# A four-layer graph network: rows of the sources found by comparison instead of a map in memory

## The reference, cut to what matters

```python
x = _layernorm(x + L0(x))   # attention over 8 heads: k[src], q[dst], softmax over edges of one dst, sum of v[src]
x = _layernorm(x + L1(x))   # two graph convolutions, with self loops and degree norm
x = _layernorm(x + L2(x))   # GAT, 4 heads: softmax over the edges of one dst, sum of h[src], elu
x = _layernorm(x + L3(x))   # two relational convolutions, 10 relations, mean per relation
```

## Time and profile before

| | us |
|---|---|
| median of 3 runs (lowest, highest) | 2712.64 (2708.06, 2718.84) |
| the profiled execution's own time | 2743.0 |
| its span | 2741.1 |
| busy in the span: PE, DVE, POOL, ACT | 2165.8, 2091.5, 1721.6, 1461.9 |

### The profile page before, as it was taken

One profiled execution on the slowest core, in us unless ns is written; L12 is line 12 of the kernel. 1 busy time (PEld: TensorE's weight loads), 2 busy tenths in 40 slices (PEclk: granted clock), 3 DMA queues, 4 the chain that ended last, 5 costly groups with the idle time before them and its releaser, 6 DMA issues. The chain is left out here.

```text
span 2741.1 us, 52605 instructions
## 1 busy us (share of the span) xinstructions
PE 2165.8 (79%) x12429; PEld 1663.7 (61%) x12429; DVE 2091.5 (76%) x7133; ACT 1461.9 (53%) x4917; POOL 1721.6 (63%) x1824
## 2 busy tenths in 40 slices
PE   2888888544878776999676999667769999899996
PEld 1766667333656665887564898456646666555553
DVE  4788888423879996887798396678868888688886
ACT  1455556233667775666454586378854444333332
POOL 3888888687877885664886687233334444355554
PEclk9999999766888997999999698788889999999998
DMA  5566666532545544554675455334432323211221
GB/s 94 173 213 211 211 206 205 110 78 66 178 156 189 177 154 162 170 173 152 189 215 185 125 183 165 99 124 129 138 122 76 84 80 84 71 51 55 57 57 31
DMA packets 294159, 369.90 MB, mean 135 GB/s; under 512 B 64976, under 2 KB 148696, under 8 KB 293858
## 3 DMA queue, kind: packets, MB, share of 16 engines
q1 hardware_dynamic: 261858, 315.33, 36.3%
q0 software_dynamic: 32000, 51.21, 7.8%
HBM read 160.78 MB, written 207.00 MB: 134 GB/s over the span
## 5 line engine op out<-in xcount | busy, mean ns | idle before, releaser
L1708 PE MATMUL phase_p_w<-phase_w_rel,phase_rowsT 128*128 128x512 f32 (+1 forms) x1200 | 510.9, 528 | 9.9 <-ACT phase_rowsT L1761 9.8
L384 PE MATMUL phase_p_h<-W2c,phase_g 128*128 128x128 f32 x1568 | 233.2, 311 | 169.9 <-ACT phase_g L339 145.5
L1789 DVE SCALAR_TENSOR_TENSOR phase_added<-phase_p_w,relation,phase_added 128x128 f32<-128x128 f32 x1200 | 350.0, 340 | 22.6 <-PE phase_p_w L1708 20.8
L324 ACT ACTIVATE phase_sq<-phase_y 128x512 f32<-128x512 f32 x294 | 186.2, 633 | 311.8 <-POOL phase_y L457 290.9
L384 PEld LDWEIGHTS phase_p_h<-W2c,phase_g 128*128 128x128 f32 x1568 | 219.9, 224 | 182.3 <-ACT phase_g L339 156.8
L656 POOL DMA_INDIRECT phase_rows<-X,src_row x200 | 192.2, 961 | 217.9 <-PE phase_p_T L1716 167.6
L978 PE MATMUL phase_p_sum<-phase_whole,phase_link 128*128 128x128 f32 (+2 forms) x792 | 183.7, 316 | 130.2 <-ACT phase_whole L1100 64.0
L656 POOL DMA_INDIRECT phase_rows<-H,src_row x200 | 193.3, 967 | 136.0 <-PE phase_p_T L1716 110.1
L345 DVE TENSOR_REDUCE phase_ss<-phase_sq 128x4 f32<-128x512 f32 x294 | 195.5, 665 | 73.8 <-ACT phase_sq L324 69.5
L1708 PEld LDWEIGHTS phase_p_w<-phase_w_rel,phase_rowsT 128*128 128x128 f32 x1200 | 189.5, 193 | 86.3 <-issue 41.1
L978 PEld LDWEIGHTS phase_p_sum<-phase_whole,phase_link 128*128 128x128 f32 x792 | 128.7, 204 | 160.5 <-ACT phase_whole L1100 78.9
(11 more groups left out here) (235 smaller groups left out, 6976.1 us busy)
## 6 DMA issues: line engine op xcount, KB each, us to landing
H<-phase_h SPq DMA_DIRECT2D x196, 256.0 KB, 3.3
X<-phase_x SPq DMA_DIRECT2D x196, 256.0 KB, 3.2
phase_same<-same_keys SPq DMA_DIRECT2D x175, 256.0 KB
phase_xT<-in_x_columns SPq DMA_DIRECT2D x98, 256.0 KB, 3.6
Z<-phase_x SPq DMA_DIRECT2D x98, 256.0 KB
phase_x<-X SPq DMA_DIRECT2D x98, 256.0 KB
out<-phase_o SPq DMA_DIRECT2D x98, 256.0 KB
H<-R SPq DMA_DIRECT2D x50, 256.0 KB, 2.4
```

The lines of the kernel that those rows point to most:

```text
L324: act.activation(self.buf(dst, g)[:, :, :], self.buf(src, g)[:, :, :], ACT.Square).then_inc(self.S[dst], 1)
L384: last = self.nc.tensor.matmul(self.P["p_h2"][:, t, :], self.buf(f"g{k}", g)[:, t, :], self.W["W2c"][:, k, :], start=(k == 0), stop=(k == 1))
L1708: nc.tensor.matmul(p_w[(PARTS * (t % UNROLL) + n) % BANKS][:, 0:b - a, :], rowsT[v][:, :], w[:, a:b, :], start=True, stop=True).then_inc(s ...
L1789: nc.vector.scalar_tensor_tensor(out=added[v][r % 2][:, :], in0=p_w[(PARTS * (t % UNROLL) + n) % BANKS][:, r % RG, :], scalar=plane(D["rel ...
```

## The change

The map goes, with its scatters, its gathers and the `slot_row` table. The sources are stored once more as floats. A new stage `source_rows`, ahead of `attention_messages`, computes `src_row` on the chip. For 512 sources at a time it loads them broadcast over 101 partitions. POOL turns the first 100 partitions into a 0/1 *step matrix*: has the tile t a first key not above the source? PE multiplies this matrix, with the plain source in the last partition, by a table of the differences of keys between neighbouring tiles and a last row of -1. The product holds, for each source, the 128 keys of the one tile in which it would stand, minus the source; a second product with a column of ones counts the tiles passed. DVE compares the first product with zero, multiplies by the ordinals 1 to 128 and takes the maximum: the last matching slot, or 0. Six small operations at the end make `src_row` of it.

The slots of dense work are dealt out anew: 112 in `source_rows` (28 steps of four), 218 in `attention_messages` as before, 24 instead of 48 in the first `weights_of_edges`, and 81 instead of 169 in `attention_rows`. In `over_all_tiles`, which all pipelined stages use except the relation ones, the step now comes before its slots.

```diff
 def over_all_tiles(step, places, dense):
     for k, slots in enumerate(places):
+        step(k)
         for i in slots:
             dense(i)
-        step(k)
...
+                sp.wait_ge(s["rows_converted"], 3)
+                sp.dma_start(io["src_f"].rearrange("(t e) -> t e", e=F), src_f[:, :]).then_inc(s["dst_stored"], 16)
                 sp.wait_ge(s["marks_full"], 2)
                 for table, marks in ((io["link_rows"], link_rows), (io["back_rows"], back_rows)):
                     sp.dma_start(table, marks[:, :]).then_inc(s["marks_stored"], 16)
-                sp.wait_ge(s["dst_stored"], 16)
+                sp.wait_ge(s["dst_stored"], 32)
...
-                sp.wait_ge(s["node_made"], 1)
-                sp.dma_start(io["row_of"].rearrange("(p n) a -> p (n a)", p=125), node[:, :]).then_inc(s["node_stored"], 16)
-                sp.wait_ge(s["node_stored"], 16)
...
-                pool.iota(node[:, :], pattern=[[1, N // 125]], base=0, channel_multiplier=N // 125).then_inc(s["node_made"], 1)
                 pool.memset(beside[:, :, :], -1).then_inc(s["beside_cleared"], 1)
-                pool.iota(D["slot_row"][:, :], pattern=[[F, T]], base=N, channel_multiplier=1)
...
+def source_rows(nc, io, W, D, beside):
+    STEPS = PASSES + 3
+    K = T + 1
+    places = beside.take(STEPS, 4 * STEPS)
+    with Phase(nc) as m:
+        keys, keys_before, starts = m.sb("keys", [T, F]), m.sb("keys_before", [T, F]), m.sb("starts", [T, 1])
+        table, tiles_passed = m.sb("table", [K, F]), m.sb("tiles_passed", [K, 1])
...
+        sources = [m.sb(f"sources{n}", [K, UNROLL, F]) for n in range(3)]
...
+        with nc.Block() as block:
+            @block.sync
+            def _(sp):
+                by_tile = io["dst_f"].rearrange("(t e) -> t e", e=F)
+                sp.dma_start(keys[:, :], by_tile).then_inc(s["keys_loaded"], 16)
+                sp.wait_ge(s["keys_cleared"], 1)
+                sp.dma_start(keys_before[1:T, :], by_tile[0:T - 1, :]).then_inc(s["keys_loaded"], 16)
+                def step(k):
+                    if k < PASSES:
+                        wait(sp, s["multiplied"], k - 2)
+                        sp.dma_start(sources[k % 3][:, :, :].rearrange("p t e -> p (t e)"),
+                                     io["src_f"][k * UNROLL * F:(k + 1) * UNROLL * F].rearrange("(a n) -> a n", a=1).partition_broadcast(K)).then_inc(s[f"sources_loaded{k % 3}"], 16)
+                over_all_tiles(step, places, lambda i: beside.dense.sp(sp, i))
+            @block.gpsimd
+            def _(pool):
+                pool.memset(keys_before[:, :], 0.0).then_inc(s["keys_cleared"], 1)
...
+                def step(k):
+                    if k < PASSES:
+                        pool.wait_ge(s["starts_full"], 1)
+                        pool.wait_ge(s[f"sources_loaded{k % 3}"], 16 * (k // 3 + 1))
+                        part = sources[k % 3][0:T, :, :]
+                        pool.tensor_scalar(part, part, starts[:, 0:1], None, ALU.is_ge).then_inc(s["steps_full"], 1)
+                over_all_tiles(step, places, lambda i: beside.dense.pool(pool, i))
+            @block.tensor
+            def _(pe):
+                def step(k):
+                    if 0 <= (j := k - 1) < PASSES:
...
+                        pe.wait_ge(s["steps_full"], j + 1)
+                        wait(pe, s["hits_full"], j - 1)
+                        for u in range(UNROLL):
+                            slots = sources[j % 3][:, u, :]
+                            nc.tensor.matmul(p_apart[j % 2][:, u, :], slots, table[:, :], start=True, stop=True)
+                            last = nc.tensor.matmul(p_passed[:, j * UNROLL + u:j * UNROLL + u + 1], slots, tiles_passed[:, :], start=True, stop=True)
+                        last.then_inc(s["multiplied"], 1)
+                over_all_tiles(step, places, lambda i: beside.dense.pe(pe, i))
+            @block.scalar
+            def _(act):
+                over_all_tiles(lambda k: None, places, lambda i: beside.dense.act(act, i))
+            @block.vector
+            def _(dve):
+                dve.wait_ge(s["keys_loaded"], 32)
+                nc.vector.tensor_copy(starts[:, :], keys[:, 0:1]).then_inc(s["starts_begun"], 1)
...
+                nc.vector.memset(starts[0:1, :], -1.0).then_inc(s["starts_full"], 1)
...
+                nc.vector.tensor_tensor(table[0:T, :], keys[:, :], keys_before[:, :], ALU.subtract).then_inc(s["table_full"], 1)
...
+                def step(k):
+                    if 0 <= (j := k - 2) < PASSES:
...
+                        dve.wait_ge(s["multiplied"], j + 1)
+                        wait(dve, s["found_full"], j - 1)
+                        nc.vector.scalar_tensor_tensor(out=hits[j % 2][:, :, :], in0=p_apart[j % 2][:, :, :], scalar=0.0,
+                                                       in1=ordinal[:, :].unsqueeze(1).to_broadcast([F, UNROLL, F]),
+                                                       op0=ALU.is_equal, op1=ALU.mult).then_inc(s["hits_full"], 1)
+                    if 0 <= (j := k - 3) < PASSES:
+                        dve.wait_ge(s["hits_full"], j + 1)
+                        nc.vector.tensor_reduce(found[:, j * UNROLL:(j + 1) * UNROLL], hits[j % 2][:, :, :], AX.X, ALU.max).then_inc(s["found_full"], 1)
+                over_all_tiles(step, places, lambda i: beside.dense.dve(dve, i))
...
+                dve.wait_ge(s["found_full"], PASSES)
+                dve.wait_ge(s["multiplied"], PASSES)
+                chained(nc.vector.tensor_scalar(passed[:, :], p_passed[:, 0:T], float(F), float(N - F - 1), ALU.mult, ALU.add))
+                chained(nc.vector.tensor_tensor(row[:, :], passed[:, :], found[:, :], ALU.add))
+                chained(nc.vector.tensor_scalar(has_slot[:, :], found[:, :], 0.5, None, ALU.is_ge))
+                chained(nc.vector.tensor_tensor(row[:, :], row[:, :], D["src_col"][:, :], ALU.subtract))
+                chained(nc.vector.tensor_tensor(row[:, :], row[:, :], has_slot[:, :], ALU.mult))
+                chained(nc.vector.tensor_tensor(D["src_row"][:, :], row[:, :], D["src_col"][:, :], ALU.add))
...
-                for k in range(STEPS):
-                    if maps:
-                        for t in range(k * UNROLL, (k + 1) * UNROLL):
-                            D["moves"].free(pool, t)
-                            pool.indirect_dma_start(out=io["row_of"], out_offset=bass.IndirectOffsetOnAxis(ap=column(D["dst_write"], t), axis=0),
-                                                    in_=column(D["slot_row"], t), in_offset=None, bounds_check=N - 1,
-                                                    oob_is_err=False).then_inc(D["moves"].sem(t), 16)
-                    until(k + 1)
-                if maps:
-                    D["moves"].all_landed(pool)
+                until(STEPS)
...
-                        moves.free(pool, t)
-                        pool.indirect_dma_start(out=column(D["src_row"], t), out_offset=None, in_=io["row_of"],
-                                                in_offset=bass.IndirectOffsetOnAxis(ap=column(D["src_col"], t), axis=0)).then_inc(moves.sem(t), 16)
                 over_all_tiles(step, places, lambda i: beside.dense.pool(pool, i))
-                moves.all_landed(pool)
...
             beside = Beside(FirstLayers(nc, m, io, W))
+            source_rows(nc, io, W, D, beside)
             attention_messages(nc, io, W, D, beside)
-            weights_of_edges(nc, io, W, D, beside, 48, (F // HEADS) ** -0.5, maps=True)
+            weights_of_edges(nc, io, W, D, beside, 24, (F // HEADS) ** -0.5)
             attention_rows(nc, io, W, D, beside)
```

More of the change, by code:

```diff
@@ L552, in prepare_edges @@
         dst_f, end_keys_apart = m.sb("dst_f", [T, F]), m.sb("end_keys_apart", [HEADS, 2, T])
-        node = m.sb("node", [125, N // 125], i32)
         attr = m.sb("attr", [F, T, RELATIONS])
@@ L557, in prepare_edges @@
         p_cols = m.pb("p_cols", [F, 3, F])
-        s = m.named("beside_cleared beside_loaded beside_converted marks_full marks_stored rows_loaded attr_loaded attr_zeroed rows_converted cols_transposed dst_stored ends_loaded node_made node_stored "
+        s = m.named("beside_cleared beside_loaded beside_converted marks_full marks_stored rows_loaded attr_loaded attr_zeroed rows_converted cols_transposed dst_stored ends_loaded "
                     "dst_col_full step_done")
@@ L755, in attention_messages, with weights_of_edges @@
         got_d.stages += 1
-def weights_of_edges(nc, io, W, D, beside, count, scale, maps):
+def weights_of_edges(nc, io, W, D, beside, count, scale):
     P = BLOCK * HEADS
@@ L906, in _ @@
                 until(STEPS)
-        if maps:
-            D["moves"].stages += 1
 LOADS = 3
@@ L1064, in attention_rows @@
         loads = TileLoads(nc, m, io, s, "summed")
-        moves = D["moves"]
         by_head = lambda a: a.rearrange("p (h d) -> p h d", h=HEADS)
@@ L1834, in gnn_kernel @@
```

(6 more changed lines are left out.)

26 lines of the change are left out of this document (added).

## The result

The changed kernel takes **2866.5 us** (median of 4 runs, 2858.1 to 2869.5) against 2715.3 us (2708.1 to 2718.8) before: ratio 1.0555, interval 1.0522 to 1.0589. It is 151 us slower; 41 us faster was forecast, and the range ended at 2725.

What follows compares the result with a forecast made beforehand. It took POOL to bound messages and weights, and DVE nearly the rows. New stage +192, messages +19, weights -127 and rows -125 made -41 us, about 2672 us against a 2712.6 us median; range 2630 to 2725 us.

Steps and rivals of the forecast that it cites:

- landing of the load: In source_rows, the time for a broadcast source load to arrive: 4.8 us, with 3.6 to 6.5 us as ends.
- The loop: In source_rows, x1, its store's issue, the next source load's landing, POOL's comparison and semaphores set the pace: 7.5 us a step.
- The comparison: In source_rows, POOL's one comparison a step, taken at 1.05 us from a two-operand operation, bounds 0.5 to 2.1 us.
- The third rival: In source_rows, the source load is late every step and the loop slower: 10.3 us a step, 2725 us in all; 15%.
- The limit of 235 us: For source_rows, the forecast counts as wrong if this new stage takes over 235 us.
- 0.45 us by the forecast's estimate: In source_rows, POOL's comparison if one-input operations run roughly at line rate; loop 6.9 us, net -52 us.
- 0 us, +-10: In over_all_tiles, swapping step and dense slots only shifts the same sequence by one step: no cost, within 10 us.
- PE at the low clock, 71 us: In the weights stage, six dense groups at PE's lower clock level throughout, with transposes and barrier: 71 us.
- DVE's term, 59 us: In the weights stage, DVE's remaining 43 us of work plus the twin's 16 us of idling: 59 us.
- 212/0.86: In the attention rows, DVE's 212 us of work at the 0.86 busy share of output rows: 246 us.
- The second rival: In the attention rows, the chain through `whole` keeps the stage at 286 us despite fewer slots: 2713 us in all; 15%.

## Why the prediction was wrong

- **New stage, 192 forecast, 348 measured.** The step that failed is "landing of the load", 4.8 us with 3.6 to 6.5 as its ends, from "a load of the same form". It is not of the same form: 101 rows against 128. The runs showed in its place a load on one DMA engine, 9.1 us with little beside it and 11.3 us in the loop. The loop, its members and its place were right, and with 128 rows the sum comes out (186.4), in part because two errors of half a microsecond cancel. The comparison, taken at 1.05 with 0.5 to 2.1 as bounds, takes 1.56. The third rival was the nearest and had the sign, but its 6.5 us came from the same rows, so its price of 10.3 us a step stayed under the 14.2 measured. The limit of 235 us, set as proof of a wrong forecast, was passed by far. The rule of the Trainium skill, "GPSIMD Engine Reference", section "Engine selection", that one-input operations run roughly at line rate there (0.45 us by the forecast's estimate) doesn't agree with the 1562 ns above.
- **Messages, 468 forecast, 480.7 measured.** With the old order 471.3, so the body was priced right, and the 9.4 us on top came with the swap, which stood at "0 us, +-10".
- **Weights, 68 forecast, 63.3 measured.** That the scatters held the stage was right. The 68 leaned on PE at the low clock, 71 us, and that term was wrong: the clock was 0.80 and not 0.70, PE was busy for 39 us, and its p_h waited for DVE's copy for 16.7 us. DVE's term, 59 us, was the nearer one.
- **Rows, 246 forecast, 268.8 measured.** The step "212/0.86" took the stage for DVE-bound. DVE is busy for 191 of 269 us, a share of 0.71. What I had expected of it did happen: the normalisation fell from 626 ns to 329. But the bound had changed to the chain of sum and `whole`, whose waits hold POOL too (935 to 1204 us):

```profile
POOL phase_message L1143 <- PE phase_p_sum L1075: 146.4, 66, 5.8
PEld phase_p_sum L1075 <- ACT phase_whole L1192: 87.8, 82, 4.9
```

The order has little part in these 23 us: with the new one and the same slots the rows take 266.1 to 268.8 us in four kernels, with the old one 265.0 to 266.5 in four others. The second rival was right in part (286): it knew the chain, and not why it is slow.
- **Sum.** Errors of +156 in the load's stage, +13 and +23 less 5 make the +186 between -41 and +145. The load is five sixths of it.

## What to carry to other kernels

Before a load's duration is borrowed from another row, check the largest divisor up to 16 of each row count; here padding 101 rows to 102 or 128 took the stage from 348 to 186 us. Slots of other work in a chain that goes back and forth between two engines can cost more than their longest engine's time when they stand alone. Try them in clusters and measure each stage by itself: it gave 47 us in one stage here and lost 28 in another. Code that only changes place in a loop is not free: it cost 16 to 20 us here.

## What the runs showed of the hardware

- A broadcast load from memory of 101 x 2 KB comes every 9.1 us beside one load of 256 KB, and in the loop it takes 11.3 us from its issue to the comparison. While it moves nearly alone the DMA share is 0.07, one engine of sixteen; with 102 rows it is 0.38, six. With 128 rows it lands in 3.0 to 4.9 us. The stage takes 185.6 us with 102 rows and 186.4 with 128.
- POOL's comparison of 100x512 with one value per partition, in place, takes 1562 ns at every step, longer than the product of two operands over 128x512 (1052 ns).
- The same stage, with the same code, took 201 to 229 us over all the traces; of the two shown, the one of 202 us has a granted clock of 0.95, the one of 229 us 0.84.
